# Ten stencil groups instead of eight summed on TensorE, and another order of outer products, additions and tap products on VectorE, in a fused deformable-convolution, attention and expert kernel

## What is computed

```python
x = x + deformable_conv(groupnorm(x))      # 3x3 points, 8 groups of 16 channels
t = x.reshape(4, 1024, 128)
t = t + attention(layernorm(t))            # softmax(t W t^T / sqrt(128)) t
t = t + experts(layernorm(t))              # two experts of eight per image, gelu, 128 -> 256 -> 128
```

```python
offset = x1 @ off_w + off_b                                  # 8*9*2 per position
mask   = softmax((x1 @ mask_w + mask_b).reshape(..., 8, 9))
out[pos, group] = sum over 9 points of mask * bilinear(xp, pos + point + offset)
```

## Time and profile before

| what | value |
|---|---|
| median of 3 runs | 676.95 us (676.77 to 677.3) |
| the profiled execution | 677.6 us, of which the span from first to last instruction is 675.7 us |
| mean granted TensorE clock | 0.970 of full speed |
| TensorE (PE) busy | 600.9 us, 89% of the span |
| VectorE (DVE) busy | 555.7 us, 82% |
| GpSimd (POOL) busy | 318.5 us, 47% |
| ScalarE (ACT) busy | 234.7 us, 35% |
| prologue and set-up | 0 to 64 us |
| seven turns | 64 to 402 us, 47.8 us each |
| chunk 7 alone | 402 to 428 us |
| attention, then experts | 430 to 600, 600 to 676 us |

### The profile page before, as it was taken

One profiled execution on the slowest core, in us unless ns is written; L12 is line 12 of the kernel. 1 busy time (PEld: TensorE's weight loads), 2 busy tenths in 40 slices (PEclk: granted clock), 3 DMA queues, 4 the chain that ended last, 5 costly groups with the idle time before them and its releaser, 6 DMA issues.

```text
span 675.7 us, 11172 instructions
## 1 busy us (share of the span) xinstructions
PE 600.9 (89%) x3668; PEld 448.7 (66%) x3668; DVE 555.7 (82%) x1028; ACT 234.7 (35%) x351; POOL 318.5 (47%) x408
## 2 busy tenths in 40 slices
PE   5989968979889889889696789999999999989995
PEld 4557556657567667666474677777777777785774
DVE  4677999999999999999999889847677766654877
ACT  6172504405207116135034000254544544415431
POOL 7504876787578588658578500202222211115222
PEclk9899989989999899899998899999999999989999
DMA  6196402103003007000000000000000000004111
GB/s 182 44 352 206 138 0 81 34 2 110 1 4 110 1 3 275 0 1 3 0 2 4 0 1 1 1 1 0 1 1 1 1 1 1 0 2 125 42 39 47
DMA packets 26244, 30.76 MB, mean 46 GB/s; under 512 B 5573, under 2 KB 18325, under 8 KB 26197
## 3 DMA queue, kind: packets, MB, share of 16 engines
q1 hardware_dynamic: 24094, 29.77, 13.4%
q0 software_dynamic: 1408, 0.36, 0.7%
q10 hardware_dynamic: 694, 0.01, 0.1%
HBM read 25.07 MB, written 5.05 MB: 45 GB/s over the span
## 4 chain that ended last, share of the span: by engine, by line
PE 44%; DVE 33%; issue 11%; ACT 2%; DVEq 0%; DMA 0%; SPq 0%; POOL 0%; ACTq 0%; POOLq 0%
DVE prod L1656 18%; PE banks L1061 9%; PE pair L1041 8%; PE banks L934 8%; DVE outer L1588 6%; PE pair L1129 4%; PE banks L1051 4%; PE banks L1167 4%; DVE hats L1539 1%; PE banks L921 1%; DVE stencil L1597 1%; PE banks L1012 1%; PE pair L864 1%; PE banks L956 1%; PE banks L1033 1%
## 5 line engine op out<-in xcount | busy, mean ns | idle before, releaser
L934 PE MATMUL banks<-ident,prod 128*128 128x128 f32 x1440 | 209.0, 288 | 44.6 <-DVE prod L1656 43.2
L934 PEld LDWEIGHTS banks<-ident,prod 128*128 128x128 f32 x1440 | 170.1, 147 | 99.4 <-DVE prod L1656 74.5
L1656 DVE TENSOR_TENSOR prod<-shifted,stencil 128x1024 f32<-128x1024 f32 (+1 forms) x208 | 216.8, 1084 | 7.6 <-ACT stencil L599 4.2
L1412 POOL TENSOR_TENSOR rstd_now<-mv_now,neg_half 128x2 f32<-128x2 f32 x32 | 23.0, 719 | 134.1 <-DVE mv_now L1704 134.1
L864 PE MATMUL pair<-xg,dw_diag 128*128 128x512 f32 x144 | 72.5, 604 | 1.4 <-DVE xg L1466 1.4
L1307 POOL DMA_INDIRECT got<-padded,cell_now x44 | 62.6, 1423 | 19.0 <-issue 10.1
L1061 PEld LDWEIGHTS banks<-shifted 128*128 128x128 f32 x512 | 60.2, 192 | 8.1 <-issue 6.1
L1061 PE MATMUL banks<-shifted 128*128 128x128 f32 x512 | 63.3, 277 | 2.3 <-ACT shifted L740 1.4
L1041 PE MATMUL pair<-shifted 128*128 128x512 f32 x128 | 60.6, 596 | 0.1
L1719 DVE TENSOR_REDUCE neg_max<-pair 128x1 f32<-128x1024 f32 x32 | 39.2, 1225 | 23.1 <-PE pair L1041 21.9
L1588 DVE TENSOR_TENSOR outer<-hats 128x800 f32<-128x800 f32 x56 | 55.5, 990 | 1.8 <-PE banks L921 1.8
(11 more groups left out here) (260 smaller groups left out, 956.4 us busy)
## 6 DMA issues: line engine op xcount, KB each, us to landing
shifted<-padded SPq DMA_DIRECT2D x42, 256.0 KB, 4.0
shifted<-padded SPq DMA_DIRECT2D x14, 640.0 KB, 8.1
res<-in_x_dram SPq DMA_DIRECT2D x4, 512.0 KB, 6.5
padded<-stage SPq DMA_DIRECT2D x4, 512.0 KB, 12.4
stage<-in_L_ffn_W_dram SPq DMA_DIRECT2D x16, 128.0 KB, 2.1
out_dram<-res SPq DMA_DIRECT2D x16, 128.0 KB, 1.8
got<-padded,cell_now POOLq DMA_INDIRECT x44, 3.0
padded<-stencil SPq DMA_DIRECT2D x2, 228.0 KB, 2.6
```

The source lines that it names most:

```text
L934: mm = pe.matmul(acc_of(c, r), prod[:, slot, r * G:(r + 1) * G, :].rearrange("p g c -> p (g c)"), ident[:, :], is_transpose=True, start=(t ...
L1656: ins = ve.tensor_tensor(prod[:, dx:dx + n, :, :], shifted[:, dx:dx + n, bass.ds(((c % HALF) * ROWS + dy) * G, ROWS * G), :], stencil_of[: ...
```

## The change

Five edits go together. `SUMMED` is 10, so TensorE sums 10 stencil groups and VectorE 22, in the prologue and in all turns. In the turns the outer product signals `outer_done` itself when it is done, VectorE's wait stands just ahead of the addition, and the units between points are split: `POINT_FILL[q]` of them stand between outer product and addition (one for q = 0, 2, 4, 6), `STENCIL_FILL[q]` behind the addition. Their sum for each q is what `POINT_FILL` was but for the shift of places, 17 units over the nine points in both. In the prologue ScalarE copies the offsets of chunk 1 before it copies the sums of chunk 0, TensorE computes these offsets after five points in place of six, and there are 16 dummy matmuls in place of 33.

```diff
-POINT_FILL = (1, 2, 2, 2, 2, 2, 2, 2, 2)
+POINT_FILL = (1, 0, 1, 0, 1, 0, 1, 0, 0)
+STENCIL_FILL = (0, 2, 1, 2, 1, 2, 1, 2, 2)
 FIRST_POINT = BEGIN + 5
-POINT_UNIT = [FIRST_POINT + sum(POINT_FILL[:q]) for q in range(PTS)]
-SUMMED = 8
+POINT_UNIT = [FIRST_POINT + sum(POINT_FILL[:q]) + sum(STENCIL_FILL[:q]) for q in range(PTS)]
+SUMMED = 10
...
             signs_of(0)
             silu(1)
             count_out(0)
-            copy_sums(0)
-            prepare(1)
+            prepare(1, sums_at=0)
             signs_of(1)
...
             count_far(0)
-            for q in range(6):
+            for q in range(5):
                 sum_point(0, q)
-                keep_clock(4, bank[3])
+                keep_clock(2, bank[3])
             offsets(1, 0, ROWS)
-            for q in range(6, PTS):
+            for q in range(5, PTS):
                 sum_point(0, q)
-                keep_clock(3, bank[3])
+            keep_clock(6, bank[3])
             add_up(0, 0, first_of(BEGIN))
...
                     if q > 0:
                         ve.wait_ge(outer_read, PTS * k + (q if q > 1 else 0))
-                    own(ve.tensor_tensor(to if q == 0 else outer[:, :, :, :],
-                                         hy[:, :, q, :].unsqueeze(3).to_broadcast(full),
-                                         hx[:, :, q, :].unsqueeze(2).to_broadcast(full), ALU.mult))
-                    own.wait()
-                    ve.sem_inc(outer_done, 1)
-                    if q == PTS - 1:
-                        ve.sem_inc(hats_used, 1)
+                    ve.tensor_tensor(to if q == 0 else outer[:, :, :, :],
+                                     hy[:, :, q, :].unsqueeze(3).to_broadcast(full),
+                                     hx[:, :, q, :].unsqueeze(2).to_broadcast(full), ALU.mult).then_inc(outer_done, 1)
+                    fill(POINT_FILL[q])
                     if q > 0:
+                        ve.wait_ge(outer_done, PTS * k + q + 1)
+                        if q == PTS - 1:
+                            ve.sem_inc(hats_used, 1)
                         to = to[:, 0:DIRECT, :, :]
                         own(ve.tensor_tensor(to, to, outer[:, 0:DIRECT, :, :], ALU.add))
-                    fill(POINT_FILL[q])
+                    fill(STENCIL_FILL[q])
                 own.wait()
```

## The result

The changed kernel takes 669.5 us (median of 4 runs, 668.86 to 671.62) against 676.92 for the kernel before (4 runs, 676.77 to 677.3). The ratio is 0.9897, 95% interval 0.9882 to 0.9913: faster, by 7.4 us. The forecast was 670.9 us. The profiled execution took 669.48 us, with a span of 667.6, so 8.1 less than the one of before.

What follows compares the result with a forecast made beforehand. VectorE's own sequence was taken to bound the turns; 677.6 less 4.0 (prologue), 1.2 (six turns) and 0.9 (turn 6) gave 671.5, less 0.65 for the median 670.9 us. Range 663.0 to 674.5, main case 668.5 to 673.5.

Steps and rivals of the forecast that it cites:

- What bounds the kernel: Turns: bound by VectorE's own sequence, busy 46.00 of 47.80 us; near ties with ScalarE's copy of the sums and TensorE.
- Prologue, a gain of 4.0: Prologue: first unit 3.3 us earlier, plus 0.7 from the vanishing wait for the hats; bounds 3.3 and 4.1.
- "61" and "70": Prologue: first unit at 61 in place of 64.27, hats at about 70 in place of 73.93.
- Turns, what VectorE saves: Turns on VectorE: 1.3 us each, four pauses 0.9 and eight shorter additions 0.4; bounds 0.4 and 1.4.
- Turns, what TensorE pays: Turns on TensorE: longer sums cost 0.8 us a turn; without a clock fall the whole 1.3 arrive, waits of 0.1.
- The clock: Turns: TensorE's clock falls just ahead of tap 28, costing 1.1 us; six turns gain 0.2 each, 1.2 in all.
- Turn 6 and the rest: Turn 6 gains 0.9 us, its low-clock wait for TensorE not seen going; chunk 7, attention and experts stay.
- The sum: Whole kernel: 677.6 - 4.0 - 1.2 - 0.9 = 671.5 us for a profiled execution; median 0.65 below, 670.9.
- The clock costs nothing: Rival, turns: clock falls earlier, before tap 21, or not at all; 663.9 us; chance 0.27.
- The prologue gives back: Rival, prologue: with half the dummies the clock falls ahead of turn 0, taking 1.7 to 3.4; 673 to 674.5; chance 0.07.
- a pause is worth nothing: Rival, turns: each gains only 0.4 and still pays 1.1 for the clock; 677 us, no change; chance 0.07.
- A clock that stays low for 10.2 us: Rival, turns from tap 28: a fall holding 10.24 us loses 3.8 a turn; 695 us, slower; chance 0.07.

Runs made afterwards that it cites:

- experiment 1: Kernel before with only SUMMED raised from 8 to 10: 676.75 us, ratio 0.9973 to the kernel before.
- experiment 2: Kernel before with the outer product signalling outer_done itself, no unit moved, eight groups summed: 674.27 us, ratio 0.9926.
- experiment 3: Kernel before with only the three prologue edits (order on ScalarE, offsets after five points, 16 dummies): 672.76 us, ratio 0.9912.
- experiment 6: Kernel before with only the units moved between outer product and addition, old signal, eight groups, old prologue: 674.64 us, ratio 0.9945.
- experiment 4: Changed kernel plus four zero-adding matmuls ahead of each of taps 21, 26 and 28: 669.93 us, ratio 0.9847 to the kernel before.
- experiment 12: Kernel before plus four zero-adding matmuls ahead of taps 21 and 28 of every turn: 677.58 us, ratio 0.9993.
- experiment 5: Changed kernel with SUMMED set back to 8: 671.21 us, ratio 0.9905 to the kernel before.
- experiment 7: Changed kernel with gate product at point 3, not 5, and its offsets from tap 21, not 30: 667.87 us, ratio 0.986 to the kernel before.
- experiment 9: Changed kernel with earlier gate product and offsets, and GpSimd's far samples left out: 659.61 us, ratio 0.9707 to the kernel before.
- experiment 10: Changed kernel with GpSimd's far samples left out: 665.81 us, ratio 0.9818 to the kernel before.
- experiment 11: Changed kernel with earlier gate product and offsets, add_fix at tap 34, not 31, projection from 37, not 35: 669.2 us, ratio 0.9886.
- experiment 8: The changed kernel itself, unedited, timed again beside others: 669.42 us, ratio 0.9905 to the kernel before.

## Why the prediction was right, point by point

- **What bounds the kernel.** Right. Experiments 1, 2, 3 and 6 each gain on VectorE's sequence or on what it waits for. They don't add: in ratio 0.27%, 0.74%, 0.88% and 0.55% are 2.4%, and the whole has 1.0%, some 9.5 us less. About 4.3 us of this are counted twice, since experiments 2 and 6 both shorten the pauses behind 0, 2, 4 and 6 (0.62 a turn). The remaining 5 or so are of the size of what the clock costs, but with intervals this wide no run shows that it is the clock alone.
- **Prologue, a gain of 4.0.** Right in its steps but one: counted from `count_far`, the first unit gained 2.8 (3.3 forecast), the hats 3.6 (4.0), and experiment 3 had 4.2. What the first unit lacks is the last sum, which starts 11.1 behind `count_far` where my 59.4 stands for 10.55: TensorE does not wait for VectorE there, as I wrote, but works from the offsets through the last four sums without a pause. The times "61" and "70" were wrong in the changed kernel's own profile, since the set-up ran 2.8 us longer, for which the forecast had no term. It is not tied to the edits as far as runs show: `count_far` starts near 48.8 in experiments 1, 4 and 12, at 49.2 to 50.3 in 5, 6, 7, 9, 10 and 11, and at 51.4 to 51.8 in 2, 3, 8 and the changed kernel. Experiment 2 has the old prologue, experiment 4 the new one. The three levels go with the time that the granted clock is at 0.50 ahead of `count_far`: 3.4 us in the first, 6.8 in the second, 10.2 in the third. Whether that goes by program or by execution is open.
- **Turns, what VectorE saves.** The term was mis-sized. Units stand directly behind outer products 0, 2, 4 and 6, additions take 0.73, and each such pause is gone, as forecast. But I let the other five pauses stay at 0.23, and the signal that the instruction itself gives makes four of them 0.11 shorter (0.15 to 0.04 behind the end) and the one behind point 8 0.09: 0.5 a turn. With 0.9 and 0.4 that is 1.8, and turn 5, with no fall, went from 47.53 to 45.85, where I had said 46.5 for a clock of 1.00. Experiment 2 shows the 0.11 alone. In the Trainium skill's page "VectorE: DVE Perf Modes", section "The DRAIN you can't avoid", a semaphore behind each of eight copies takes no time. For an addition that needs the product in front, the rows here speak against carrying that over: 0.12 for the wait (0.04 behind the end against 0.08 before it), and another 0.11 for the wait and the separate signal by the sequencer.
- **Turns, what TensorE pays.** Right for full clock, but for a wait of 0.2 (turn 5) to 0.4 (experiment 4) for the copy of the sums where I had 0.1. That ten groups in place of eight bring nothing measurable (experiment 5) was not foreseen; I had 0.4 a turn less the sums' cost.
- **The clock.** The mechanism was right, and the place nearly. In turns 0 to 4 the clock falls at the start of tap 28: 0.6 ahead of it in turn 0, with it in turn 1, and 0.6 to 0.9 behind it in turns 2 to 4. In turn 3 the waits before it are 1.21 at tap 21, 1.12 at tap 26, 0.41 at sum 5 and 1.22 at tap 28 (1.4, 1.3, 0.6 and 1.5 forecast), and VectorE pays 0.90 at outer product 8 and 0.51 at the copy, besides 0.40 at 7. The size was low: turn 5 against turns 0 to 3 gives 1.3 to 1.7, experiment 4 gives 1.2 to 1.7, and I took 1.1. That was the middle between a low stretch that lies wholly in work (1.7) and one that begins ahead of the last wait (0.6); in turns 1 to 4 it lies wholly in work. I also had it in all six turns, and it came in five, in turn 0 for 6.8 us and not 3.4. The two errors of size nearly cancel in a turn with a fall: 1.8 less 1.5 is about 0.3, and turns 1 to 4 gained 0.3 to 0.6, as against the 0.2 of the forecast.
- **Turn 6 and the rest.** Too low: 3.6 in place of 0.9. The wait of 1.75 for TensorE, "which I don't see going", is gone, and with the 1.8 of VectorE this is the 3.6. The clock is low for 6.8 us in turn 6 where it was 10.2 before. In experiments 4 and 7, where it is low for 10.2 again, the wait is back at 1.93 and 1.76, and turn 6 and chunk 7 gain 1.6 and 2.0. So half of this gain hangs on where the clock falls, which I had not forecast.
- **The sum.** 8.1 in the profiled executions against 6.1 forecast (4.0 + 1.2 + 0.9). Up to the hats of turn 0 it is 0.75 against 4.0, from there to turn 6 3.9 against 1.2, in turn 6 and chunk 7 3.6 against 0.9. The total came close by luck in part: the longer set-up, 2.8, stood against a gain in the turns that I had too small.
- **The rivals.** "The clock costs nothing" is out by the turns of experiment 4. "The prologue gives back" is out by experiment 3, "a pause is worth nothing" by experiments 2 and 6. A clock that stays low for 10.2 us was not seen in turns 0 to 5 of the changed kernel, where the longest is 6.8; experiment 7 has one in turn 4, around the wait for GpSimd.

## What to carry to other kernels

Take the completion signal from the instruction that makes the data, and put independent work between it and its reader: a point then loses neither the 0.11 of the separate signal nor the 0.12 of the wait. When such an edit takes idle time out of the bounding engine, ask where the other engine's waits now lie: the same low clock of 3.4 us cost nothing where slack followed (tap 21 before, turn 0 of experiment 10) and about 1.4 us ahead of a stretch without a wait. And count what each turn hands to the slow engine behind the others; here the gain of four turns came out again as one wait of 5.7 or 7.7 us for GpSimd in the fifth.

## What the runs showed of the hardware that I had not expected

- On VectorE an instruction that reads the result of the one in front starts 0.15 us behind its end with a wait in the sequencer and a separate signal, and 0.04 with the instruction's own signal. Other work put between starts 0.08 before the end.
- Four matmuls ahead of a tap whose moving operand is one column of zeros, read 128 times, hold the granted clock at 1.00 in turns 0 to 5, where it else falls to 0.50 (all but turn 4 of experiment 4, where TensorE waits 5.71); in turn 6 it falls all the same. They add nothing to a turn of the kernel before, where VectorE is the bound (experiment 12: 47.78 against 47.84 in turn 3).
- The set-up of one and the same program text, up to `count_far`, lasts 48.8 to 51.8 us between kernels that don't differ there. The granted clock of 20 to 24 us is 0.86 before and 0.52 after, and it is at 0.50 for 3.4 us in the shortest set-ups and for 10.2 us in the longest.
- Leaving GpSimd's samples out made the clock fall in three turns in place of five, though VectorE and TensorE do the same work (experiment 10).
